# Constant products on TensorE at six places of a two-layer attention and experts kernel

## The reference

```python
x = x + windowed_attention(ln(x))          # 14x14 windows, 12 heads of 16, relative positions, softmax
t = t + experts0(ln(t))                    # router: softmax over 8, top 2; gelu(x W1 + b1) W2 + b2
x = x + dilated_attention(ln(x))           # 3x3 neighbours at dilations 1, 2, 3
t = t + experts1(ln(t))                    # as above, the two gates scaled to sum 1
```

## Time and profile before

| | |
|---|---|
| median of 3 runs | 969.56 us (966.18 to 976.19) |
| profiled execution | 964.97 us |
| its span, first to last instruction | 963.1 us |
| mean granted TensorE clock over the span | 0.847 |
| PE busy | 731.6 us (76%), weight loads 623.2 us (65%) |
| VectorE busy | 472.7 us (49%) |
| GpSimd busy | 451.4 us (47%) |
| ScalarE busy | 284.9 us (30%) |

### The profile page before, as it was taken

How to read it: one execution, slowest core, us unless ns; L and a number is a source line. 1 busy time by engine, 2 the same in 40 slices (tenths; PEclk the granted TensorE clock), 3 DMA queues, 4 the chain that set the end, 5 groups by cost and what they waited for, 6 DMA issues and landing times.

```text
span 963.1 us, 18777 instructions
## 1 busy us (share of the span) xinstructions
PE 731.6 (76%) x5822; PEld 623.2 (65%) x5823; DVE 472.7 (49%) x1007; ACT 284.9 (30%) x812; POOL 451.4 (47%) x823
## 2 busy tenths in 40 slices
PE   2899999999846999999814622553585499999990
PEld 1777888888635999999813410121275499999990
DVE  7124464566455333333265079999264633333324
ACT  3323454545311333333312300000121133333330
POOL 5853343410214666666433243884221366666641
PEclk9665999999957999999957755977775699999996
DMA  6582564652931111111030496000393011111115
GB/s 210 140 206 72 123 154 110 161 124 54 365 136 32 45 49 45 47 53 48 27 131 27 137 215 112 0 22 23 106 369 125 28 45 47 49 48 49 48 32 197
DMA packets 66119, 96.58 MB, mean 100 GB/s; under 512 B 29182, under 2 KB 50514, under 8 KB 66070
## 3 DMA queue, kind: packets, MB, share of 16 engines
q1 hardware_dynamic: 47318, 61.79, 22.8%
q0 software_dynamic: 18752, 34.15, 11.9%
HBM read 65.61 MB, written 31.52 MB: 101 GB/s over the span
## 4 chain that ended last, share of the span: by engine, by line
PE 60%; DVE 24%; issue 5%; POOL 4%; DMA 3%; ACT 2%; SPq 1%; DVEq 0%; POOLq 0%; ACTq 0%
PE ps L1366 13%; PE ps L1374 10%; PE ps L1378 6%; DVE rt L1639 5%; PE ps L736 4%; PE ps L718 3%; PE ps L762 3%; DVE x_sb L1315 2%; DVE arena L1632 2%; DVE xn L1632 2%; PE ps L375 2%; DVE xn L296 2%; PE ps L746 2%; PE ps L1357 2%; PE ps L1699 2%
## 5 line engine op out<-in xcount | busy, mean ns | idle before, releaser
L1406 ACT ACTIVATE arena<-ps,b1s 128x128 f32<-128x128 f32 x468 | 129.5, 375 | 264.7 <-PE ps L1378 177.4
L1366 PE MATMUL ps<-arena 128*128 x936 | 165.4, 327 | 1.5 <-DVE rt L1282 1.5
L1366 PEld LDWEIGHTS ps<-arena 128*128 128x128 f32 x936 | 150.3, 190 | 2.4 <-issue 2.1
L1374 PE MATMUL ps<-xnT 128*128 128x128 f32 x936 | 120.1, 279 | 4.3 <-DVE xnT L1275 4.3
L1374 PEld LDWEIGHTS ps<-xnT 128*128 128x128 f32 x936 | 116.8, 195 | 5.5 <-DVE xnT L1275 5.5
L1420 POOL TENSOR_TENSOR credit<-credit 1x1 f32<-1x1 f32 x306 | 57.5, 188 | 78.6 <-DVE rt L1282 34.3
L1709 PE MATMUL ps<-xnT,cst 128*128 128x512 f32 (+3 forms) x88 | 44.6, 639 | 65.0 <-POOL xnT L1591 65.0
L598 DVE TENSOR_REDUCE rt<-ps 98x2 f32<-98x392 f32 x96 | 52.8, 561 | 77.8 <-PE ps L762 77.8
L1591 POOL TENSOR_TENSOR xnT<-arena,rt 128x1024 f32<-128x1024 f32 (+3 forms) x21 | 66.4, 3186 | 48.3 <-DVE rt L1666 36.7
L1428 POOL DMA_INDIRECT xnT<-xnd,gcur x78 | 79.0, 1012 | 15.9 <-issue 14.7
L1709 PEld LDWEIGHTS ps<-xnT,cst 128*128 128x128 f32 x88 | 16.7, 209 | 93.5 <-POOL xnT L1591 81.1
(11 more groups left out here) (202 smaller groups left out, 1306.7 us busy)
## 6 DMA issues: line engine op xcount, KB each, us to landing
arena<-in_w SPq DMA_DIRECT2D x16, 576.0 KB, 8.2
arena<-in_w1a SPq DMA_DIRECT2D x16, 384.0 KB, 6.4
arena<-yd SPq DMA_DIRECT2D x8, 768.0 KB, 6.7
kk<-kd SPq DMA_DIRECT2D x48, 96.0 KB
qq<-qd SPq DMA_DIRECT2D x16, 264.0 KB
qd<-arena POOLq DMA_DIRECT2D x16, 224.0 KB, 5.5
qq<-qd SPq DMA_DIRECT2D x16, 192.0 KB
arena<-in_w1b SPq DMA_DIRECT2D x16, 192.0 KB, 6.5
```

What stands on the lines that cost most here:

```text
L1366: last = mm(ps[:, DOWN, 0:C], hidT[r][:, f, :], w2s[:, e, f, :], start=f == 0, stop=f == FT - 1)
L1374: mm(hidden(r, f), wcura[r][:, f * P:(f + 1) * P], xgT[:, 0, :], start=f < 2, stop=False, skip_group_check=True)
L1406: last = nc.scalar.activation(hidT[r][:, f, :], hidden(r, f), ACT.Gelu, bias=b1s[l][:, bass.ds(e * FT + f, 1)])
```

## The change

TensorE gets matmuls of constant or unused data whose results nobody reads. VectorE first writes ones into 512 unused columns of `rt`. The wait for the constants moves from before the prologue to behind nine products of this tile. The others use constants already there (`ident` and `cst`, float32; `trib` and `maskb`, bf16). Targets are PSUM banks that are free at that point; for one of them (bank 5) a wait is added.

```diff
+            filler = rt[:, 2304:2304 + BT]
+            def keep_clock(bank, n):
+                for _ in range(n):
+                    mm(ps[:, bank, :], filler[:, 0:P], filler, start=True, stop=True)
...
+            pe.wait_ge(s_("filler_ready"), 1)
+            keep_clock(BANK["r2", 0], 9)
+            pe.wait_ge(s_("cst_in"), 16)
             for k in range(2):
                 transposes(0, k)
...
             queries_and_keys(0, 1)
+            keep_clock(BANK["r2", 0], 2)
             relatives(0, 2)
...
+            pe.wait_ge(s_(EMPTIED["r1", 0][0]), EMPTIED["r1", 0][1])
             for H in range(AHEAD):
                 for u in range(UNITS):
                     scores_for_max(H, u)
+                    mm(ps[:, PV, 0:2 * P], trib, maskb[:, 0, 0:2 * P], start=True, stop=True)
...
             last.then_inc(s_("ranks_mm"), 1)
+            for _ in range(6):
+                mm(ps[:, 0, :], ident, cst[:, 0:BT], start=True, stop=True)
             for c in range(COLS):
...
             last.then_inc(s_("tables_mm"), 1)
+            for _ in range(4):
+                mm(ps[:, 0, :], ident, cst[:, 0:BT], start=True, stop=True)
...
+            for _ in range(15):
+                nc.tensor.matmul(ps[:, 6, :], ident, cst[:, 0:BT], start=True, stop=True)
             for b in range(BLKS + 1):
                 if b < BLKS:
                     transpose(b)
...
         def _(v):
+            nc.vector.memset(rt[:, 2304:2304 + BT], 1.0).then_inc(s_("filler_ready"), 1)
             ln_moments(v, 0, first)
...
         def _(pe):
-            pe.wait_ge(s_("cst_in"), 16)
             attn0_tensor(pe)
```

## The result

The changed kernel takes 965.29 us (median of 20 runs, 958.93 to 970.81) against 970.57 us for the kernel before (20 runs of the same session): ratio 0.9937, 95% interval 0.9914 to 0.9960. That is 5 to 6 us faster where 13 were forecast. Rival 1 had given 965.5; rivals 2 and 3, at 963.9 and 963.2, lie inside the interval too (962.2 to 966.7), so the time alone does not choose among them. The profiled execution took 960.46 us.

The account below looks back on a forecast made before the run. TensorE was taken as always busy but at half clock in stretches of the first 98 us; 0 - 6.5 + 1.0 - 7.0 - 2.6 + 2.0 = -13.1 us from the 969.56 median gave 956 us, range 949 to 974.

Parts of the forecast that it names:

- Rival 1: Only the prologue gains, as the maxima warm too late or the loop cools at once: 965.5 us, chance 0.20.
- rivals 2 and 3: 2: only maxima and loop gain, 963.9 us, chance 0.10; 3: warm-up worth little, other engines set pace, 963.2 us, chance 0.13.
- Two products: Prologue, after the second set of queries: two products raise the clock for the work that follows, -6.5 us.
- the relative positions at 58.28 get less of the warm time: +0.8: Prologue, block 1: relative positions get less warm time than their 7.03 us had, costing 0.8 us.
- the -2.7 for them: Prologue: the queries of block 1 run warm, 6.15 becoming 3.4 us, 2.7 saved.
- not 8.8: Prologue after the two products: warm 64-row relative positions, values, transposes and block 1's queries together save 8.8 us.
- The loads "late next": Prologue: loads of the third and fourth chunk, started by SyncE at 57.52, come no sooner; 1.2 us taken off the gain.
- The nine: Start of the prologue: nine products end before PE's first real work and the clock is lost again, 0 us.
- The maxima: Units of the first maxima: eighteen products cost +1.0 us, with the clock rising after about 5 us.
- The loop: Loop behind the maxima, cold from 74.4 to 98 us, runs warm: -7.0 us, the large term.
- Routers: Both routers, six and four products each: first expert tiles start warm, -2.6 us in sum.
- Fifteen: Second attention, while its values travel: fifteen products end 3.7 us late, warm work wins back 1.6, net +2.0 us.

Follow-up runs that it names:

- fill_relatives: Changed kernel with three bf16 products of 256 columns after each of the eight pieces of block 1's relative positions in the prologue: 963.54 us, 0.9932.
- no_nine: Changed kernel without the nine products of the prologue: 960.88 us, 0.9919 of the kernel before.
- ten: Changed kernel with ten products instead of fifteen while the values of attention 1 travel: 959.5 us, 0.9891 of the kernel before.
- no_routers: Changed kernel without the six and four products in both routers: 969.48 us, 0.9986 of the kernel before.
- only_two: Kernel before with only the two products after the second set of queries, plus their waits and write of ones: 965.71 us, 0.9959.
- combined_no_loop: The combined kernel without any products in the loop: 953.47 us, 0.9847 of the kernel before.
- after_again: Changed kernel, unchanged, profiled once more: single run of 966.55 us.
- fill_loop: Changed kernel with two bf16 products of 256 columns behind each unit of heads 0 to 3 of the loop: 963.05 us, 0.9945.
- fill_reorder: fill_relatives with the first negated maxima sent before the fourth chunk's loads instead of behind them: 959.96 us, 0.9914 of the kernel before.
- the combined kernel: Changed kernel without the nine, relative positions filled, negated maxima before fourth chunk's loads, two products a unit in loop heads 0 to 3, ten for fifteen: 954.77 us, 0.9857.

## Why the prediction was wrong

**Two products, -6.5 forecast.** The profile gave -1.4 for the whole prologue, and the mean over the eight profiles that have these products and unchanged relative positions is 62.0 against 65.7 before: -3.7. The warm rows came as priced. In the pair of profiles the line "the relative positions at 58.28 get less of the warm time: +0.8" failed: they lost 3.7 us, because the clock, raised 16 us sooner, was gone 1.6 us into them. By the means it is spread wider, because I took one profile's clock for the kernel's. The two profiles of before start these relative positions at 57.3 on average, and their queries of block 1 took 6.15 and 3.70 us, so part of the -2.7 for them was there already. The 64-row relative positions started 1.8 us later and not 0.3, the stretch between was 6.7 us shorter and not 8.8, and the relative positions 1.1 longer. fill_relatives shows what a full clock there is worth: 6.8 sooner, 6.0 on average.

**The loads "late next", 1.2 taken off.** The right wait: 0.45 to 1.75 us for the negated maxima in five of the eight profiles with maxima from 60.8 us on, none in the other three, and 3.8 us once they began at 58.3. Its remedy was one line.

**The nine, 0 forecast.** Right, by the mechanism named: they end at 12.2, the clock is at half from 17.3.

**The maxima, +1.0 forecast.** +0.9 in the profile, the clock was raised 4.7 us after their start. That the products are its cause is not shown: without them the stage was no shorter.

**The loop, -7.0 forecast.** -4.6 to head 4 in the pair of profiles, and 0.7 lost again in the last heads. Most of the -4.6 is a draw. From the loop's first scores to the third exponential of head 4, the two profiles of before take 24.5 and 22.0 us, and the five of kernels with this loop and its maxima products (both of the changed kernel, no_nine, ten, no_routers) 19.8, 23.0, 21.3, 22.4 and 24.7: -1.0 on average. The price was right (11.4 us for the three steps where the clock is full throughout). The step that failed is that the clock, once full, stays so. Of the 14 profiles of changed kernels 13 had it full at the end of the maxima or early in the loop, and 12 of them lost it between 71.0 and 82.1 us; only_two never had it there.

What takes it there is not shown. I had the narrow matmuls of four heads as the cause, but in five of the twelve (fill_relatives, combined_no_loop, after_again, no_routers, ten) the first fall came before the loop's first narrow matmul. In all twelve PE had stood idle for 0.8 to 3.8 us, for a transfer or for GpSimd's copy, during the fall or at most 2.6 us before it. fill_loop had such a wait too (1.5 us) and kept the clock. No run takes the waits away alone.

The loop (6.0 us less than forecast) and the two products (2.8 less) are the miss. The other terms came near.

**Routers, -2.6 forecast.** -2.8 by the table of points; the first tile of layer 0 came 0.1 late and not 0.4. **Fifteen, +2.0 forecast.** +2.2, and ten instead give -1.5.

**Rival 1** had the direction right, a gain in the prologue and none behind it, and its 965.5 was the time. Its terms were not: -6.5 for the prologue and +3 for the maxima and the loop, a figure it gave no rows for, where the means are -3.6 and 0 in the five profiles named. The two errors cancel, so that the number fits is partly luck.

The Trainium skill's sentence on the ramp ("TensorE: Matmul & The Clock Gate", Part 1: The HAM clock gate: under 1% of a typical span) is kept by the changed kernel's gain, 0.6%. It speaks of a ramp from a cold start, and here the clock falls again in several stages, so it does not bound what there was to win: the combined kernel without products in the loop is 1.5% faster, though up to 0.4% of this may be the turned order, by the 3.9 us that fill_reorder's loop starts sooner.

## What to carry to other kernels

Products that raise TensorE's clock pay where dense work follows directly (routers: 1.3 us or more in each layer, for 1.1 and 1.5 priced) and must end before what they bridge to arrives. Count them at the clock they will run at. Before a long stream of narrow matmuls a raise was soon lost again, unless wider products stood among them. In a stage where TensorE waits now and then, products among its work did not hold the clock in three profiles of four. One profile is one draw of where the clock changes: take two or three of the kernel before, and as many of the changed one, before a stage's duration is called a bound or a gain.

## What the runs showed of the hardware

Being busy does not keep the full clock. With PE busy 13.4 of 13.4 us and weight loads 12.98 (54.9 to 68.3 us) it was at half; with 24 products of 256 columns strewn among the same matmuls it was full from 36.8 to 71.0, and so through this stretch in six profiles of six. A unit of the first maxima with its product took PE 0.57 us at half clock (65.48 to 66.05 us in the changed kernel), a head's third unit 0.64 (64.84 to 65.48), where I had counted 0.63. And the clock is not fixed in time even where nothing was changed: the narrow matmuls of block 1 took 7.03 and 10.32 us in two profiles of the kernel before.
